# Attention value products turned around: decay blocks stationary, 64 value columns moving

## What is computed

```python
log_D = log_fg_matrix + ig[:, :, None, :]
D = jnp.exp(log_D - max_log_D)                 # lower triangle, else 0
k_hop = jnp.einsum('bhvc,vmhc->bhvm', qh, pe)  # pe = rpe[hops]: a row per (query, key)
C = (qk + k_hop) * D
Cn = C / (normalizer + EPS)
h = Cn @ vh                                    # the value product
hn = (h - mu) / jnp.sqrt(var + LN_EPS)
```

## Time and profile before

| what | value |
|---|---|
| median of 3 runs | 3314.08 us |
| the profiled execution | 3310.51 us |
| its span, first to last instruction | 3308.5 us, 69970 instructions |
| around the span | 2.0 us |
| mean granted TensorE clock | 0.964 of full |
| busy: TensorE / its weight loads | 2938.0 us / 1856.5 us |
| busy: VectorE / GpSimd / ScalarE | 2417.6 / 2023.2 / 1941.4 us |

### The profile page before, as it was taken

The page is one execution under the profiler, slowest core; times in us unless marked ns, Lnnn a source line. Parts: engine busy times, 40 slices in busy tenths (PEclk is TensorE's granted clock), DMA queues, the critical chain, the costliest instruction groups (busy, mean ns, idle before and its releaser), DMA issues.

```text
span 3308.5 us, 69970 instructions
## 1 busy us (share of the span) xinstructions
PE 2938.0 (89%) x24660; PEld 1856.5 (56%) x24660; DVE 2417.6 (73%) x5103; ACT 1941.4 (59%) x4654; POOL 2023.2 (61%) x2195
## 2 busy tenths in 40 slices
PE   6777777777777777699999999999999999999998
PEld 4555454544544554366666666666666666666664
DVE  5655555555555555588888888888888888888875
ACT  3444444444444444477666676666766767667663
POOL 6777777777777777256455455564554645546554
PEclk8888899999999999799999999999999999999999
DMA  9999999999999999556556565565565655656542
GB/s 283 345 349 349 320 348 344 344 352 352 347 345 346 351 348 326 190 184 189 180 174 185 178 189 179 177 187 181 177 190 169 195 173 179 187 179 180 185 148 66
DMA packets 414909, 799.98 MB, mean 242 GB/s; under 512 B 107338, under 2 KB 213834, under 8 KB 412516
## 3 DMA queue, kind: packets, MB, share of 16 engines
q1 hardware_dynamic: 312516, 453.08, 43.6%
q0 software_dynamic: 82560, 270.60, 24.5%
q10 hardware_dynamic: 19488, 71.84, 5.6%
HBM read 618.02 MB, written 176.69 MB: 240 GB/s over the span
## 4 chain that ended last, share of the span: by engine, by line
PE 65%; DMA 16%; POOL 9%; issue 5%; DVE 4%; ACT 1%; SPq 0%; POOLq 0%; DVEq 0%; ACTq 0%
DMA arena<-in_L_xattn_rpe_dram,arena 15%; PE psum L1772 13%; PE psum L1689 9%; PE psum L1701 9%; PE psum L1724 9%; PE psum L1627 7%; PE psum L1600 6%; POOL arena L797 6%; PE psum L1616 4%; PE psum L1753 3%; PE psum L1776 3%; PE psum L1664 2%; POOL arena L782 2%; PE psum L1569 1%; DVE arena L1237 1%
## 5 line engine op out<-in xcount | busy, mean ns | idle before, releaser
L797 POOL DMA_INDIRECT arena<-in_L_xattn_rpe_dram,arena x768 | 731.8, 953 | 235.0 <-issue 181.6
L1600 PE MATMUL psum<-arena 128*128 128x128 f32 x4128 | 614.4, 297 | 190.3 <-DMA arena<-in_L_xattn_rpe_dram,arena 178.6
L1600 PEld LDWEIGHTS psum<-arena 128*128 128x128 f32 x4128 | 488.9, 151 | 422.9 <-DMA arena<-in_L_xattn_rpe_dram,arena 292.9
L993 ACT ACTIVATE arena<-arena 128x512 f32<-128x512 f32 (+3 forms) x1024 | 496.3, 555 | 43.7 <-PE psum L1724 39.2
L1772 PE MATMUL psum<-arena 128*128 128x512 f32 x1024 | 493.3, 595 | 0.0
L1347 DVE TENSOR_TENSOR arena<-psum,arena 128x1024 f32<-128x1024 f32 (+1 forms) x384 | 386.6, 1041 | 133.3 <-PE psum L1701 122.4
L573 DVE COPY arena<-psum 128x512 f32<-128x512 f32 x384 | 263.4, 689 | 239.3 <-PE psum L1600 235.5
L582 DVE COPY arena<-psum 128x416 f32<-128x416 f32 (+15 forms) x512 | 225.3, 442 | 278.4 <-PE psum L1616 270.1
L823 POOL TENSOR_SCALAR_AFFINE_SELECT arena<-arena 128x256 f32<-128x256 f32 x256 | 118.7, 464 | 503.9 <-ACT arena L993 491.6
L1616 PE MATMUL psum<-arena 64*32 64x416 f32 (+7 forms) x8192 | 361.5, 422 | 59.3 <-ACT arena L909 38.1
L573 ACT COPY arena<-psum 128x512 f32<-128x512 f32 x384 | 225.8, 588 | 251.7 <-PE psum L1600 248.7
(11 more groups left out here) (112 smaller groups left out, 4632.1 us busy)
## 6 DMA issues: line engine op xcount, KB each, us to landing
arena<-in_x_dram SPq DMA_DIRECT2D x256, 256.0 KB, 4.1
arena<-gate_rows SPq DMA_DIRECT2D x128, 512.0 KB, 4.4
arena<-in_x_dram SPq DMA_DIRECT2D x512, 64.0 KB
arena<-in_ctx_dram SPq DMA_DIRECT2D x32, 1024.0 KB, 7.5
out_dram<-arena SPq DMA_DIRECT2D x128, 256.0 KB, 2.9
arena<-in_L_xattn_rpe_dram,arena POOLq DMA_INDIRECT x1032, 7.1
arena<-hop_products SPq DMA_DIRECT2D x128, 128.0 KB, 2.6
arena<-hop_products SPq DMA_DIRECT2D x128, 120.0 KB, 2.5
```

The costliest lines, as they stand in the source:

```text
L797: nc.gpsimd.indirect_dma_start(out=rows[set_of(n, v)][:, t, :], out_offset=None, in_=rpe[:, :], in_offset=bass.IndirectOffsetOnAxis(ap=her ...
L993: last = nc.scalar.activation(decay[u % DECAYS][:, e, at:at + width], top_pair[p % 2][:, e * S + j * P:e * S + j * P + width], ACT.Exp, bi ...
L1600: last = nc.tensor.transpose(turn_bank(o)[:, q * P:(q + 1) * P], own[:, q * P:(q + 1) * P], ident)
```

## The change

The decay block becomes the stationary operand (128 keys x 128 queries) and the 64 value columns of one head move. A unit of 4, 4 or 2 blocks gives 8, 8 or 4 products, each issued as two pairs. The result lands with queries on partitions, in the layout that `pair_out` reads, so `pair_turned`, `turn_back`, the tile `attT`, the semaphore `pe_o` and the table `BACK` go. For pair 0, `pair_out` takes the place where `pair_turned` stood on ScalarE, ahead of `ffn_norm(rf, 0)`; the other three stay where they were. On VectorE the sums of pair 0 move ahead of `value_means(2)`.

```diff
-        BACK = {2: 0, 3: 1, 5: 2}
-                def pair_turned(r, p):
-
-                    act.wait_ge(pe_a.sem, pe_a.done(r.b, ("value", 3 * p + 2)))
-                    act.wait_ge(pe_o.sem, pe_o.done(r.b, ("back", (p - 1) % 4), 1 if p < 1 else 0))
-                    nc.scalar.copy(attT, bank(pair_bank(p))).then_inc(act_o.sem, act_o.step(("turned", p)))
                 def pair_out(r, p):
                     got = bank(pair_bank(p)).rearrange("p (t e c) -> p t e c", t=ST, e=HPT)
-                    act.wait_ge(pe_o.sem, pe_o.done(r.b, ("back", p)))
+                    act.wait_ge(pe_a.sem, pe_a.done(r.b, ("value", 3 * p + 2)))
...
                 if ra:
-                    pair_turned(ra, 0)
+                    pair_out(ra, 0)
                 if rf:
                     ffn_norm(rf, 0)
...
                     value_means(1)
+                if ra:
+                    pair_sums(ra, 0)
+                if rp:
                     value_means(2)
-                if ra:
-                    pair_sums(ra, 0)
...
-                    for n, (j, at, width) in enumerate(RUNS[k]):
-                        for e in range(HPT):
-                            last = nc.tensor.matmul(psum[e * DH:(e + 1) * DH,
-                                                         pair_bank(p) * BANK + j * P:pair_bank(p) * BANK + j * P + width],
-                                                    values[ra.par][:, j, HPT * p + e, :],
-                                                    decay[u % DECAYS][:, e, at:at + width],
-                                                    start=(k == 0 and n == 0), stop=True, skip_group_check=True)
+                    out = bank(pair_bank(p)).rearrange("p (i e c) -> p i e c", i=ST, e=HPT)
+                    for j, at, width in RUNS[k]:
+                        for n in range(width // P):
+                            for e in range(HPT):
+                                last = nc.tensor.matmul(out[:, j + n, e, :],
+                                                        decay[u % DECAYS][:, e, at + n * P:at + (n + 1) * P],
+                                                        values[ra.par][:, j, HPT * p + e, :],
+                                                        start=(k == 0 and n == 0 and e == 0), stop=True,
+                                                        skip_group_check=True)
                     last.then_inc(pe_a.sem, pe_a.step(("value", u)))
-                def turn_back(r, p):
-                    pe.wait_ge(act_o.sem, act_o.done(r.b, ("turned", p)))
-                    turn(pair_bank(p), attT).then_inc(pe_o.sem, pe_o.step(("back", p)))
```

More of the change, by code:

```diff
@@ L221, in build @@
         decay = [place(HPT * 4 * P).rearrange("p (e c) -> p e c", e=HPT) for _ in range(DECAYS)]
-        attT = place(S)
         att = [place(ST * DIM).rearrange("p (t h c) -> p t h c", t=ST, h=NH) for _ in range(2)]
@@ L435, in build @@
         pool_a = Stage(sem("pool_a"), [("mask", u) for u in units])
-        act_o = Stage(sem("act_o"), [(n, p) for p in pairs for n in ("turned", "copy", "square")])
-        pe_o = Stage(sem("pe_o"), [("back", p) for p in pairs])
+        act_o = Stage(sem("act_o"), [(n, p) for p in pairs for n in ("copy", "square")])
         dve_o = Stage(sem("dve_o"), [(n, p) for p in pairs for n in ("sum", "sq_sum")] +
@@ L1092, in run @@
                     second_weight(rg, 3)
-                if rf:
-                    pair_turned(rf, 3)
                 if ra:
@@ L1134, in run @@
                 if ra:
-                    pair_out(ra, 0)
                     unit_decay(ra, 6)
@@ L1140, in run @@
                     second_weight(rf, 0)
-                if ra:
-                    pair_turned(ra, 1)
                 if rp:
@@ L1179, in run @@
                     second_weight(rf, 2)
-                if ra:
-                    pair_turned(ra, 2)
                 if rf:
@@ L1492, in run @@
                     value_means(1)
-                    value_means(2)
                 if ra:
                     pair_sums(ra, 0)
+                if rp:
+                    value_means(2)
                 if rf:
@@ L1542, in _ @@
             pe_q.start(pe)
-            for st in (pe_p, pe_a, pe_o, pe_f):
+            for st in (pe_p, pe_a, pe_f):
                 st.start(pe)
@@ L1786, in run @@
                     if d == 0:
-                        if rf:
-                            turn_back(rf, 3)
                         if rp:
@@ L1803, in run @@
                         turn_ffn(rf, 0)
-                    if ra and d in BACK:
-                        turn_back(ra, BACK[d])
                     if rp and d == 2:
```

## The result

The changed kernel takes 3517.74 us (3516.01 to 3518.54, three runs) against 3314.08: 6.1% slower, ratio 1.0614, interval 1.0599 to 1.0629. The forecast was 3509 us, the range 3478 to 3562.

The account below looks back on a forecast made before the run. TensorE's instruction stream was taken to bound the batch loop: 17.27 - 9.54 - 1.32 - 0.05 - 0.10 = +6.26 us a round, +200 over 32 rounds, less 5 = +195, 3505.8, plus 3.6 to the median: 3509 us, range 3478 to 3562.

Parts of the forecast that it names:

- What bounds the kernel: Batch loop: a steady round lasts exactly as long as TensorE's stream of instructions, 59.88 us.
- The pace of a pair: Value products: each load-and-multiply pair takes 0.110 us, between 0.108 and 0.117, with 160 pairs a round.
- The short end of a stretch and the gap at its entry: Six value-product stretches: the short last multiply takes off 0.33 us a round; the gap on entering falls away.
- `gates`: After the sums of pair 0, which come earlier after the change: 0.1 us a round off, between 0 and 0.1.
- The turns back: Four removed on TensorE, 0.44 us each; those at d = 3, d = 5 and d = 0 save 1.32 in all.
- the one at d = 2: Turn back beside ScalarE's two copies ahead of the routes: removing it saves 0.05 us, between 0 and 0.44.
- my cover, VectorE's multiply: Before the value products at d = 3 and d = 5: VectorE's multiply ends early enough to leave room for 0.44 us.
- `pair_out(0)` ahead of the norm: ScalarE: the norm comes 0.6 us later, covered by the value products of d = 1; uncovered it would cost 19 us.
- The edges: First attention round and last round: idle time swallows 5 us of the addition, between 0 and 15.
- a load at 0.061 us: Rival, value products: 128-column loads follow each other after 0.061 us; -51 us, about 3263 us; chance 0.05.
- a load that isn't hidden: Rival, value products: loads wait for the multiply ahead, 0.165 us a pair; +477 us, 3791 us; chance 0.05.
- The falling clock: Rival, value stretches: clock drops to 1.2 GHz, 17.3 us more a round, near 4060 us; chance 0.03.

Follow-up runs that it names:

- e3_halves: The changed kernel with each 128-query block split into two stationary halves of 64 queries on different array columns, everything computed; 3314.4 us, 0.9981 of the kernel before.
- e12: The changed kernel with the first 96 of each block's 128 queries stationary, the last 32 left out; 3384.9 us, one run.
- e1: The changed kernel with only 32 of the 64 value columns of each head moving in the value products; 3608.9 us, ratio 1.0869.

## Why the prediction was right

- *What bounds the kernel*: TensorE's stream, before and after. The round rose by 6.54 us against the forecast 6.26. Before, a round also held two short waits, 0.03 us each: `gate_stats` for `gate_floor` and `gates` for the sums of pair 0.
- *The pace of a pair*: forecast 0.110 us within 0.108 to 0.117, measured 0.1115. This term was mis-sized by 0.0015 us, 0.24 a round, 8 us in all. I took the gap between two loads at the start of a stretch of L1753. In a row of load-bound pairs there are some 5 ns a pair on top of the columns.
- *How near the time came*: from one profiled execution to the other 207 us were added where 195 were forecast. Of the missing 12, 9 lie in the rounds (8 of them in the pace) and 3 at the edges. That 3518 is only 9 us above 3509 has some luck in it: I added 3.6 us for the distance from the profiled execution to the median, and after the change the profiled execution is the median.
- *The short end of a stretch and the gap at its entry*: both as said. The last multiply counts 0.05 less, and the products begin right behind routes and transposes; the old 0.09 us at the entry comes back in the halves, which divide the array again.
- *`gates`*: 0.1 us a round, as said. Its piece was 0.03 + 1.92 us in the chain of the kernel before and is 1.85 now.
- *The turns back*: the one at d = 2 was forecast at 0.05 us. From the turn of `queries(2)` to the end of the routes the chain takes 1.85 + 1.02 = 2.87 us before and 2235.81 to 2238.63, so 2.82, after. As said, the routes still go by the copy of the turned rows: their first load starts 0.05 us after it ends, at 2208.10 before and at 2237.36 after. What I hadn't named is that the turn of `queries(3)` now waits 0.34 us for the copy of `queries(2)` in the same place. That at d = 5 is worth all of its time. That at d = 3 is worth all of it only because the longer products give VectorE time; in the kernel before some of it would have been lost, which my cover, VectorE's multiply, didn't show. I had looked at the wrong wait of that stretch: it is `gate_stats`, not the value product. That at d = 0 was not tested by itself; the sum of the round (17.56 - 9.54 - 1.32 - 0.05 - 0.10 = 6.55) leaves nothing missing.
- *`pair_out(0)` ahead of the norm*: covered, as said. The list of waits of the changed kernel's loop has L970 alone, 8.4 us in 25 rounds (part of the 2.82 above). In e3_halves, without the long products of d = 1, the list has 5.5 us for the norm in the same order.
- *The edges*: -5 us forecast, -2.1 measured (the span grew by 207.2 us, 32 x 6.54 is 209.3), and not where I put it. The first attention round didn't swallow any of the addition in its idle time: it grew by 6.8 us, with the granted clock at 0.92 in the stretch that had 1.00 before. The second grew by 4.0 and the tail by 6.7, the steady rounds by 6.54, and two rounds of the kernel before had been 0.9 longer than the rest.
- *The rivals*: a load at 0.061 us and a load that isn't hidden are excluded by the pace of 0.1115 us, which e12 and e1 give to the load's columns. The rule of the Trainium skill, TensorE: Matmul & The Clock Gate, Part 3, that a load overlaps multiplies only for another row group, doesn't hold here: the same rows and columns were in use, and multiplies of 64 and of 32 columns both vanished under the load. The falling clock didn't come with 64 moving columns, but with 32 it did; my chance of 0.03 was for a danger that was nearer than the traces of before could show.

## What to carry to other kernels

Which operand is stationary decides what a float32 product costs: in these runs a pair takes the longer of its load (its stationary columns) and its multiply (its moving columns), so a block with few moving columns behind a full load pays for the load. Before an orientation is turned to save a transpose, count the array's columns: two products that ran side by side in half the columns each are worth more than the transpose (8.0 us a round against 1.4 here), and if the result can be written in halves on different partitions, both can be had, once what waits behind the shorter stream is moved. A step taken off the bounding engine is worth its length only where the next engine has room: read each wait that follows it, not only the nearest.

## What the runs showed of the hardware that I hadn't expected

- A load-bound float32 pair takes 0.83 ns a stationary column plus some 5 ns (111.5, 85 and 58.4 ns for 128, 96 and 64), while multiply-bound transposes pace at 109 ns for 128 columns.
- TensorE can be busy for 99.5% of the time in the profile and still be granted the lower clock: 147 us of the 1650 between 1480 and 3130 us with 32 moving columns behind each full load, 27 with 48, none with 64 (one profile each).
- Weight loads of different columns of the array run side by side, two of 64 columns in the time of one. Going from the full array to products of 64 stationary columns costs 0.09 us at each entry; with 96 it costs nothing.
- With 20480 load-and-multiply pairs in quarters TensorE stood idle now and then with nothing to wait for, up to 3.5 us at a time; the cause is open.
